# Differential attention with two PSUM banks for a head's sums and two for odd jobs, in place of one and three

## What is computed

```python
xn = layernorm(x)
q = rotary(rmsnorm((xn @ Wq.T).reshape(B, T, 16, 16)))
k = rotary(rmsnorm((xn @ Wk.T).reshape(B, T, 16, 16)))
v = (xn @ Wv.T).reshape(B, T, 8, 32)
a = softmax(mask(q @ k.T / 4))            # causal, one for each of 16 half heads
att = a[even] @ v - lam * (a[odd] @ v)    # one for each of 8 heads
out = (1 - lambda_init) * layernorm_of_head(att)
x = x + out @ Wproj.T
```

## Time and profile before

| | us |
|---|---|
| median of 3 runs | 4453.76 (4449.64 to 4458.86) |
| profiled execution | 4466.52 |
| its span, first to last instruction | 4464.7 |
| TensorE busy | 3727.2 (83%) |
| VectorE busy | 2867.2 (64%) |
| ScalarE busy | 1911.5 (43%) |
| GpSimd busy | 1574.8 (35%) |
| mean granted TensorE clock | 0.916 |

### The profile page before, as it was taken

The page is one execution under the profiler, slowest core; times in us unless marked ns, Lnnn a source line. Parts: engine busy times, 40 slices in busy tenths (PEclk is TensorE's granted clock), DMA queues, the critical chain, the costliest instruction groups (busy, mean ns, idle before and its releaser), DMA issues. The chain is left out here.

```text
span 4464.7 us, 60005 instructions
## 1 busy us (share of the span) xinstructions
PE 3727.2 (83%) x19288; PEld 2571.7 (58%) x19288; DVE 2867.2 (64%) x5347; ACT 1911.5 (43%) x3864; POOL 1574.8 (35%) x1463
## 2 busy tenths in 40 slices
PE   5888877996799999987997688876885888888898
PEld 3455466885588888876786244444663333333566
DVE  5777555664555555455564577877884566664898
ACT  3556542432455545543442444422221455555222
POOL 4676535443665556435443111100002333330000
PEclk8899988998899999987999798897997699998999
DMA  5999712555000000002555000000002454450000
GB/s 137 275 288 238 237 39 88 161 161 160 10 17 14 11 10 11 1 30 82 156 161 173 24 12 17 19 1 15 0 0 51 87 103 80 97 101 15 9 10 19
DMA packets 221650, 348.36 MB, mean 78 GB/s; under 512 B 34632, under 2 KB 126266, under 8 KB 215226
## 3 DMA queue, kind: packets, MB, share of 16 engines
q1 hardware_dynamic: 198714, 260.66, 19.9%
q0 software_dynamic: 22656, 84.24, 8.3%
HBM read 166.29 MB, written 169.87 MB: 75 GB/s over the span
## 5 line engine op out<-in xcount | busy, mean ns | idle before, releaser
L2780 DVE TENSOR_REDUCE ab_nmx<-banks 128x1 f32<-128x512 f32 x512 | 334.7, 685 | 222.0 <-PE banks L2596 221.0
L1673 POOL TENSOR_TENSOR lb_pq<-lb_pq,lb_rr 128x512 f32<-128x512 f32 x192 | 204.4, 1068 | 308.0 <-DVE lb_rr L1552 305.0
L2722 ACT ACTIVATE ab_pt<-banks 128x512 f32<-128x512 f32 x512 | 273.8, 600 | 91.3 <-PE banks L2606 79.8
L2606 PE MATMUL banks<-ab_qT,ab_kT 49*128 49x512 f32 x512 | 231.6, 499 | 55.6 <-ACT ab_pt L2722 51.9
L1427 ACT ACTIVATE lb_pq<-banks,lb_nmx 128x256 f32<-128x256 f32 x384 | 178.9, 471 | 220.5 <-DVE lb_nmx L1547 217.4
L2596 PE MATMUL banks<-ab_kT,ab_qT 48*128 48x512 f32 x512 | 239.3, 515 | 31.2 <-DMA ab_kT<-ab_spill 19.1
L1547 DVE TENSOR_REDUCE lb_nmx<-banks 128x2 f32<-128x512 f32 x192 | 131.5, 685 | 186.0 <-PE banks L1279 185.0
L2606 PEld LDWEIGHTS banks<-ab_qT,ab_kT 49*128 49x128 f32 x512 | 93.8, 197 | 267.6 <-ACT ab_pt L2722 158.7
L358 ACT ACTIVATE da_pt<-banks 128x512 f32<-128x512 f32 (+1 forms) x384 | 179.1, 540 | 120.2 <-PE banks L270 116.4
L643 POOL DMA_INDIRECT mb_xi<-moe_ys,moe_b_place x64 | 63.5, 993 | 391.0 <-DVE mb_uT L2054 343.0
L285 PE MATMUL banks<-da_pt,da_vx 128*64 128x512 f32 (+3 forms) x1024 | 167.7, 473 | 29.9 <-POOL da_pt L577 26.1
(11 more groups left out here) (561 smaller groups left out, 11461.1 us busy)
## 6 DMA issues: line engine op xcount, KB each, us to landing
moe_xs<-zero SPq DMA_DIRECT2D x71, 512.0 KB, 11.5
moe_ys<-zero SPq DMA_DIRECT2D x71, 512.0 KB, 11.2
moe_a_w_raw<-in_moe_w SPq DMA_DIRECT2D x48, 512.0 KB, 4.7
moe_b_w_raw<-in_moe_w SPq DMA_DIRECT2D x48, 512.0 KB, 4.5
da_spill<-da_hi SPq DMA_DIRECT2D x128, 128.0 KB, 2.4
ab_spill<-ab_hi SPq DMA_DIRECT2D x128, 128.0 KB
da_qT<-da_spill POOLq DMA_DIRECT2D x32, 384.0 KB, 7.1
da_kT<-da_spill POOLq DMA_DIRECT2D x32, 384.0 KB, 10.7
```

The lines of the kernel that those rows point to most:

```text
L1673: nc.gpsimd.tensor_tensor(pq[:, n % RING, :, :], pq[:, n % RING, :, :], bcast(rr[:, n % RING, :], 2, 2 * P), ALU.mult).then_inc(s_p, 1)
L2606: nc.tensor.matmul(ps[:, EXP_BANK + n % 3, :], kT[b % 2][r:r + AB_ROWS + 1, p, j * P:(j + 1) * P], qT[b % 2][r:r + AB_ROWS + 1, p, :], sta ...
L2722: nc.scalar.activation(pt[:, s % RING, :], ps[:, EXP_BANK + s % 3, :], ACT.Exp, scale=AB_D ** -0.5).then_inc(s_e, 1)
L2780: nc.vector.tensor_reduce(nmx[:, g % 2, col:col + 1], ps[:, MAX_BANK + n % 3, :], op=ALU.max, axis=AX.X, negate=True).then_inc(s_mx, 1)
```

## The change

The second sums bank is taken from the odd jobs. `ODD_BANK` goes from 5 to 6 and `NODD` from 3 to 2, so job n takes bank 6 + n mod 2 and waits for the job two before it. Head hv's sums go to bank 4 + hv mod 2, and `values` waits for the copy of head hv - 2 in place of head hv - 1. ScalarE reads the bank of its head. Nothing else differs: the same instructions in the same order on every engine.

```diff
-    S_BANK, AV_BANK, ODD_BANK, NODD = 0, 4, 5, 3
+    S_BANK, AV_BANK, ODD_BANK, NODD = 0, 4, 6, 2
...
-                    if hv >= 1:
-                        pe.wait_ge(s_osb, hv)
+                    if hv >= 2:
+                        pe.wait_ge(s_osb, hv - 1)
...
-                            last = nc.tensor.matmul(ps[64 * sub:64 * sub + 64, AV_BANK, j * P:T],
+                            last = nc.tensor.matmul(ps[64 * sub:64 * sub + 64, AV_BANK + hv % 2, j * P:T],
...
-                    nc.scalar.copy(osb[:, hv % 2, :], ps[:, AV_BANK, :]).then_inc(s_osb, 1)
+                    nc.scalar.copy(osb[:, hv % 2, :], ps[:, AV_BANK + hv % 2, :]).then_inc(s_osb, 1)
```

## The result

The changed kernel takes 4494.98 us (median of 5 runs, 4492.13 to 4512.82) against 4453.76 for the one before (5 runs): ratio 1.0107, 95% interval 1.0080 to 1.0133. It is slower by about 1.1% or 41 us (33 were forecast), inside the stated range.

A forecast was written before the change was run, and what follows sets the result against it. TensorE was taken to set the pace up to slot 11, a VectorE and GpSimd chain behind it. The terms -2.5 + 10.0 + 15.5 + 4.5 + 2.4 + 1.0 - 2.0 + 5.0, say +33, gave 4487 us, range 4468 to 4504.

The forecast's parts named there:

- Rival 1: Most of the delay, in slots 5 and 2, is swallowed before slot 11: +8.5, 4462 us, chance 0.10.
- Part A: Second sums bank: the values product no longer waits for ScalarE's sums copy, -2.5 us, bounds 0 and -5.
- Part B: Slots 15 and 0: out1 itself waits for out0's bank, v0 behind it; 2.0 us in five turns, +10.0 us.
- Part G: Granted clock falls to its lower level after idle gaps, chiefly before out1: +5 us, bounds 0 and 21.
- Parts C and D: Slot 5: qk0 waits for back0's bank, +15.5 us; slot 2: x1 waits for turn0's bank, delaying back, +4.5 us.
- Part E: Slot 13: back waits 1.2 us for heads0's bank; swallowed in five turns, lost in the last two, +2.4 us.
- Part F: Single places, a back before v1 and the last row's turn: +1.0 us, between 0 and 3.
- what was to be taken up: Small waits for GpSimd and ScalarE before slot 11 absorb part of the delay: -2.0 us for six turns.
- rival 3: Clock takes its upper bound: pauses of 2 to 4 us, two a turn, keep it low; +49, 4503 us, chance 0.16.

The follow-up runs named there:

- out_earlier: Changed kernel with both out jobs moved to slot 14, ahead of VectorE's rotary work: stage ends at 616.6 us, ratio 1.0086 to the kernel before.
- one_sum_two_odd: Kernel before with odd jobs on two banks, sums still on one, bank 5 unused: stage ends at 620.3 us, ratio 1.0106.
- second pair: Kernel before and changed kernel, both unaltered, profiled again: stage ends at 577.2 and 619.7 us.
- warm: one_sum_two_odd with dummy transposes into unused bank 5 ahead of five kinds of waiting fills: stage ends at 605.3 us, ratio 1.0059 to the kernel before.
- spare_out1: one_sum_two_odd with unused bank 5 given to the out1 jobs alone: stage ends at 614.4 us, ratio 1.0092 to the kernel before.

## Why the prediction was right

**Carrying over.** TensorE set the pace before slot 11 and VectorE's chain behind it, as said. The section from the root to out0's free bank is 26.6 us in both kernels and in every experiment but out_earlier: what happened before the root moved the whole turn, and what happened in slot 13 was swallowed. Rival 1 is refuted: the turns grew by 5.8 to 8.5 us.

**Part A** (-2.5): what was priced is there (0.13 us a head in six late heads, 0.3 to 0.5 us in each of five turns), and a fall of the clock behind the seventh row's heads job takes it back. The sum is 0 within 2.5 us, in two profiles each with and without it.

**Part B** (+10 in five turns): the five waits of L332 are there. v0 comes 3.22 us later behind the free bank, not 2.0; out1 runs at the lower clock and so takes longer. Its five waits are 4.35 to 6.25 us long, where G had 2.5 to 4.4 in four turns.

**Parts C and D** (+3.0 and +0.8 a turn): together 3.68 us in the section from turn0 to qk0, against 3.8.

**Part E**: about 1.1 us seven times, swallowed in five turns. In the last two it was not: in the sixth row the job ahead of it in slot 13 began 39.6 us later than in the kernel before and the back 40.9 us later, in the seventh 43.2 and 44.5.

**Part F and what was to be taken up** (+1.0, -2.0): the single places were not isolated. The small waits took up nothing. Between qk0 and the heads of slot 13, TensorE is idle for 14.2 us in five turns before and 14.0 in one_sum_two_odd.

**Part G** (+5): this is the term that was mis-sized. Busy time of the stage grew by 22.8 us for the same matmuls, against the 5 taken and an upper bound of 21. Summed over the five turns, 6.9 us of it lie between qk0 and slot 13 and 6.1 in out1 (7.0 and 5.9 in the second pair of profiles). These 13 us are at the two places that G named. Another 3.3 us (5.0 in the second pair) lie from slot 13 to out1 and 7.5 (1.9) behind the last v0, which G did not name; the other stretches sum to -1. Not all of it is on the path, as slot 13 and the values product behind it (4.2 to 4.5 in place of 2.4 to 3.2 us) lie in the swallowed stretch. warm puts what reaches the end at 15 us.

I had priced the fall behind out1's wait alone as likely. In the profile after it falls in each of the five turns at three places: behind qk0's stall, in slot 13, and behind out1's wait. Before, it fell one to three times a turn, in slot 13, behind the gap before L285 or at v0, and never behind qk0. The rows held a warning that the prediction left out. It took the 2.37 us gap before v0 as harmless, but behind one of 2.40 us, before the v0 at 402.06, the clock fell 1.3 us later, in the same trace:

```profile
403.40:406.80 3.40, 3.40 (x16) 2.95 (x16) 3.16 (x11) 1.74 (x4) 1.11 (x2) 0.50 0.88 161
```

The prediction's own bound of rival 3 (+49) was nearer the measured stage (+45.7) than the forecast (+33.9). Waits, +28.9 in the sum of the other parts, came out at +22.9 of idle time. That is net of what the gap before L285 lost. What the waits cost on the path is better read from warm, whose stage ends 28.8 us behind the kernel before (605.3 against 576.5); the parts of the sum that warm has, without A and G, were +31.4. So the waits were sized about right and the clock at a third of its 15 us, and the forecast is short by about 12 us in the stage. The median's +41 lies just inside the forecast's own range, +22 to +43; the stage's +45.7, and +42.5 in the second pair, are beyond its end and at it. That the whole kernel came nearer to the forecast than the stage is scatter of the later stages and not to the forecast's credit. (The sum was 33.9 and was put down as 33.)

**What was to be seen**: the stage was to end at about 610 and a turn to last 69 us; they are 622 and 71.6. L285's wait for L577 was to stay near 26 us and is 10.7, because I forgot my own part E there: what that gap swallows, it loses. Part E is 5.5 of these 15.4 us, most of the rest is the lower clock in slot 13. The named waits of L332, L316 and L138 came as said.

The Trainium skill's rule that groups of matmuls should rotate through different banks (Perfetto Trace Analysis, section Matmuls) is borne out for the odd jobs, whose third bank is worth about 40 us of the stage. For the sums the waits go as it says, and nothing is left of it at the stage's end. Which kind needed the bank was to be read from the trace: the sums' bank was waited for 2.8 us in all, the odd banks over 19.

## What to carry to other kernels

Before a buffer is moved from one ring to another, compare for each instruction the time at which it starts with the time at which the buffer it would then get came free; the few places with a positive difference, here five of the 24 jobs of a turn, are the cost. A wait that is added ahead of an existing one on the same buffer costs the work that used to run inside the wait. On an engine that sets the pace, price each new pause twice, once as time and once as lower clock: here the lower clock was about a third of the loss by warm (15 of 44 us) and half of it by TensorE's busy time.

## What the runs showed of the hardware that was not expected

The granted clock can fall to its lower level behind pauses that are short but close together. In the changed kernel idle stretches of 1.08 and 2.22 us with 0.6 us of work between them were followed by a clock of 0.56 from 309.1 to 312.6; before the change 0.78 us in that place was followed by a clock of 1.00. In both profiles of the changed kernel the clock falls there in all five turns. Single pauses of nearly the same length went either way: behind 2.37 us the v0 of one row ran at full clock, behind 2.40 us that of another had the clock fall 1.3 us after its start. Behind 3.98 us in spare_out1 v0 ran at the lower clock from its first matmul. Of the rule in the Trainium skill (TensorE: Matmul & The Clock Gate, section What's actually happening) that activity is what releases the throttle, warm is the test in this case, and it agrees: transposes whose result nobody reads kept the clock of the five turns at 0.95 to 0.98 in place of 0.88 and 0.89, and shortened the stage by 15 us.

The price of a pause depends on the others. The banks for out1 and qk0 brought 5.9 and 18.1 us alone and 31.7 us together, and the excess of 7.7 us, three times the 2.5 us by which profiles of one kernel differ, is all in TensorE's busy time. So the parts of such a change can't be timed one by one and added.
